# One-hot compares and the coupled sweep's outer-product multiplies, divided along the five tiles of a block

## The chip, the cores and the metric

The kernel runs on one core of a Trainium2 chip. The metric is the device time of one execution in microseconds; lower is better. A program on one core, launched once.

## The reference

Four graph layers follow each other on 12,500 nodes with 32 features (8 scalars and 8 vectors of 3) and 400,000 edges, whose targets `dst` are sorted and whose sources `src` are random. After each layer `x = layernorm(x + layer(x))`.

```python
# layers 0 and 3: weights of each edge from a small network of its own features
w = mlp(edge_features)                       # 4 x 8 x 8 numbers an edge
msg = contract(x[src], edge_harmonics, w)    # 32 numbers an edge
out = segment_sum(msg, dst) + x @ own
...
# layer 1: fixed coupling, harmonics of order 0, 1 and 2 (1 + 3 + 5 = 9 numbers an edge)
msg = sum_paths(W[path], CG[path], sh[path], x[src])
out = segment_sum(msg, dst)
...
# layer 2: two graph convolutions
out = relu(segment_sum(norm * (x @ W)[src], dst) + b)
```

## The kernel before

There are five sweeps over all edges, each followed by a short stage over the nodes: `weighted_edges` (called `weighted0`), `coupled_edges`, `conv_edges` twice, and `weighted_edges` again (called `weighted3`). A program-wide barrier stands between stages. Edges come in blocks of 640, that is 5 tiles (`TILES`) of 128 (`P`), one edge a partition; there are 628 blocks (625 real, padded to 157 turns of `SLOTS` = 4). Since targets are sorted, the targets of one block lie within 64 consecutive nodes (`WINDOW`), so one pass over the blocks is enough for these inputs.

What a block goes through in each sweep:

- SP (`load_blocks`, L301) loads the block's source indices and, where there are any, harmonics and features, into one of four slots. It refills slot s as soon as the messages of that slot's block are made (semaphore `msg_ready`; in the convolutions `spread`).
- POOL (`gather_rows`, L323) issues five indirect DMAs a block, one a tile, that fetch the rows `x[src]` from HBM into `rows[s]`. Each reads a column of indices in SBUF.
- DVE makes a one-hot matrix of each edge's target within the window (`Windows.one_hot`, L359): a compare of `iota` (64 columns) with the local target of the edge, for five tiles in one instruction. It stands at the start of the block's work, ahead of the waits for the gather.
- DVE makes the messages. In `coupled_edges` these are two multiplies: the outer product of the first four harmonics with the 32 features (L701, 5 x 128 columns) and of the other five with the 24 vector features (L705, 5 x 120 columns). In `weighted_edges` there are eleven instructions between the one-hot and `msg_ready` (L576 to L613), of which L594 and L599 read PE's weights in PSUM. In `conv_edges` there are none; PE takes the gathered rows.
- PE multiplies the messages by the one-hot and sums the five tiles in PSUM (L492, L669, L753). In `weighted_edges` PE also makes each edge's weights (L446, L448, L458); there its order is written out by hand: hidden layer of block n + 2, weights of n + 1, then the sum of block n.
- DVE adds the window's sums into the accumulator `acc` in SBUF (`add_window`, L560, L688, L767), at a column that it reads from a register.

All orders are those of the code: each engine's queue runs in program order, and a semaphore count is the only link between engines. DVE's order in a turn of four blocks in `coupled_edges` is: read the bases (L366), then for each slot the one-hot, the wait for gather and loads, the two multiplies, and the add of the block before.

## Time and profile before

| | us |
|---|---|
| time, median of 3 runs | 26496.01 |
| lowest and highest | 26398.16, 26498.13 |
| span of the profiled execution | 21541.2 |
| median less span | 4954.8 |
| busy in the span: PE, DVE, ACT, POOL | 13199.4, 9294.4, 2665.2, 15690.7 |

The span is the time from the first to the last instruction that the profiler recorded in one execution; the profile gives no other time of that execution, so the median stands for it. The times by stage, from the slices of the page: the first weighted sweep takes slices 1 to 8, the coupled sweep 9 to 16, the convolutions 17 to 32, the last weighted sweep 33 to 40. Node stages are short. "Issue" as a releaser means that the engine waited for nothing that the profile shows.

### The profile page before, as it was taken

Reading aid. Unit: us, or ns where it says so; the run is one execution under the profiler, and the core shown is the slowest. Engines: PE = TensorE matmul, PEld = TensorE weight load, DVE = VectorE, ACT = ScalarE, POOL = GpSimd, SP = SyncE. Lnnn points to the kernel's source line nnn. Section 1 sums busy time; section 2 is a strip of 40 time slices with the busy share of each in tenths; the row PEclk is TensorE's granted clock in tenths of the full one; section 3 lists DMA queues with packets and bytes.
Section 4 is the critical chain, followed back from the end, with each engine's and each line's share of the span. In section 5 each row is a group of like instructions: output and inputs, shape, how many; then the busy total and the mean of one; then the engine's idle time right before and its main releaser. Section 6 shows DMA issues by size and latency. Waiting matters only on the chain. (4 is left out here: it accounts for less than half of the span.)

```text
span 21541.2 us, 268058 instructions
## 1 busy us (share of the span) xinstructions
PE 13199.4 (61%) x71680; PEld 9916.4 (46%) x71680; DVE 9294.4 (43%) x22443; ACT 2665.2 (12%) x6512; POOL 15690.7 (73%) x15707
## 2 busy tenths in 40 slices
PE   8999999976666666512222223212221399999999
PEld 5666666666666666511111112111111266666666
DVE  7777777833333333211111111111111388888885
ACT  2333333310000000100000000000000022222222
POOL 6777777747777777677777774777777677777774
PEclk8988988955555555555555555555555599999997
DMA  1111111111111111100000010000000111111111
GB/s 32 26 26 26 26 26 26 27 13 16 16 16 16 16 16 16 15 14 14 14 14 14 14 13 12 14 14 14 14 14 14 15 17 18 18 17 18 17 17 13
DMA packets 1290570, 372.67 MB, mean 17 GB/s; under 512 B 1002127, under 2 KB 1269819, under 8 KB 1290172
## 3 DMA queue, kind: packets, MB, share of 16 engines
q0 software_dynamic: 502400, 258.23, 7.7%
q1 hardware_dynamic: 788150, 114.20, 3.3%
q8 instruction: 8, 0.13, 0.0%
q14 instruction: 12, 0.10, 0.0%
HBM read 363.02 MB, written 8.00 MB: 17 GB/s over the span
## 5 line engine op out<-in xcount | busy, mean ns | idle before, releaser
L323 POOL DMA_INDIRECT conv_rows<-conv_rows,conv_idx x6280 | 5927.4, 944 | 2245.2 <-issue 1912.6
L753 PE MATMUL conv_win<-conv_onehot,conv_rows 128*32 128x64 f32 x12560 | 1572.6, 312 | 6305.3 <-DMA conv_rows<-conv_rows,conv_idx 6254.9
L753 PEld LDWEIGHTS conv_win<-conv_onehot,conv_rows 128*32 128x32 f32 x12560 | 1298.6, 169 | 6579.0 <-issue 4974.1
L323 POOL DMA_INDIRECT coupled_rows<-x_after_weighted,coupled_idx x3140 | 3302.0, 1052 | 1206.1 <-issue 955.0
L323 POOL DMA_INDIRECT weighted_rows<-in_x,weighted_idx x3140 | 3251.5, 1036 | 1105.3 <-issue 937.4
L323 POOL DMA_INDIRECT weighted_rows<-x_after_convolved,weighted_idx x3140 | 3209.0, 1022 | 1064.2 <-issue 953.7
L458 PE MATMUL weighted_weights_ps<-weighted_w_out,weighted_hidden 128*128 128x256 f32 x12580 | 3781.5, 426 | 21.1 <-DVEq L550 21.1
L669 PE MATMUL coupled_win<-coupled_onehot,coupled_prod 128*125 128x64 f32 x12560 | 2762.0, 418 | 1531.0 <-DVE coupled_prod L705 1531.0
L669 PEld LDWEIGHTS coupled_win<-coupled_onehot,coupled_prod 128*125 128x125 f32 x12560 | 2677.4, 330 | 1615.6 <-issue 834.5
L458 PEld LDWEIGHTS weighted_weights_ps<-weighted_w_out,weighted_hidden 128*128 128x128 f32 x12580 | 2256.0, 199 | 1818.0 <-issue 1617.9
L767 DVE TENSOR_TENSOR acc<-acc,conv_win 32x64 f32 x1256 | 262.3, 209 | 6237.3 <-PE conv_win L753 6237.3
L492 PEld LDWEIGHTS weighted_win_ps<-weighted_onehot,weighted_prod 128*128 128x128 f32 (+1 forms) x25120 | 2463.5, 166 | 522.2 <-issue 262.6
L492 PE MATMUL weighted_win_ps<-weighted_onehot,weighted_prod 128*128 128x64 f32 (+1 forms) x25120 | 2542.1, 254 | 242.8 <-DVE weighted_prod L613 241.4
L594 DVE TENSOR_TENSOR weighted_v_v<-weighted_weights_ps,weighted_scaled 128x320 f32<-128x320 f32 x3768 | 1966.0, 577 | 127.0 <-ACT weighted_scaled L520 123.0
L448 PE MATMUL weighted_hid_ps<-weighted_feat,weighted_w_in 32*64 32x320 f32 (+1 forms) x3780 | 1543.6, 489 | 95.9 <-DMA weighted_feat<-in_ef 78.6
L701 DVE TENSOR_TENSOR coupled_prod<-coupled_sh,coupled_rows 128x640 f32<-128x640 f32 x628 | 518.3, 825 | 1726.5 <-DMA coupled_rows<-x_after_weighted,coupled_idx 1726.5
L599 DVE TENSOR_TENSOR weighted_to_s<-weighted_weights_ps,weighted_scaled 128x640 f32<-128x640 f32 x1256 | 1020.6, 813 | 0.0
L446 PE MATMUL weighted_hid_ps<-weighted_first,weighted_w_mid 128*64 128x320 f32 x2520 | 953.3, 460 | 2.8 <-ACT weighted_first L505 2.1
L359 DVE TENSOR_TENSOR conv_onehot<-conv_iota,local 128x320 f32<-128x320 f32 x1256 | 589.8, 490 | 786.0 <-issue 786.0
L508 ACT ACTIVATE weighted_hidden<-weighted_hid_ps,weighted_b_in 64x320 f32<-64x320 f32 x1260 | 657.5, 522 | 1808.6 <-PE weighted_hid_ps L448 1806.4
L520 ACT ACTIVATE weighted_scaled<-weighted_rows,weighted_sh 128x32 f32<-128x32 f32 x3140 | 732.5, 309 | 1133.9 <-DMA weighted_rows<-in_x,weighted_idx 1116.7
L587 DVE TENSOR_TENSOR weighted_s_v<-weighted_weights_ps,weighted_rows 128x320 f32<-128x320 f32 x1256 | 613.6, 489 | 564.2 <-PE weighted_weights_ps L458 554.3
(133 smaller groups left out, 8636.9 us busy)
## 6 DMA issues: line engine op xcount, KB each, us to landing
conv_rows<-conv_rows,conv_idx POOLq DMA_INDIRECT x6280, 2.3
weighted_feat<-in_ef SPq DMA_DIRECT2D x632, 80.0 KB
weighted_rows<-in_x,weighted_idx POOLq DMA_INDIRECT x3140
coupled_rows<-x_after_weighted,coupled_idx POOLq DMA_INDIRECT x3140, 2.3
weighted_rows<-x_after_convolved,weighted_idx POOLq DMA_INDIRECT x3140, 2.3
weighted_idx<-in_src_blocks SPq DMA_DIRECT2D x1264, 2.5 KB
weighted_sh<-in_sh SPq DMA_DIRECT2D x1264, 10.0 KB
conv_idx<-in_src_blocks SPq DMA_DIRECT2D x1264, 2.5 KB, 1.6
```

Of the source, the lines that this page charges most:

```text
L323: pool.indirect_dma_start(rows[s][:, t, :], None, table, bass.IndirectOffsetOnAxis(ap=idx[s][:, t:t + 1].bitcast(U32), axis=0))\
L446: mm = pe.matmul(hid_ps[0:HID, 0:HALF], w_mid[:, u - 1, :], first[:, :], start=True, stop=True)
L448: mm = pe.matmul(hid_ps[0:halves * HID, 0:HALF], w_in[:, :], feat[slot][:, u * HALF:(u + 1) * HALF], start=True, stop=True)
L458: mm = pe.matmul(banks[bank][:, t * WPATHS:(t + 1) * WPATHS], hidden[slot][:, t * P:(t + 1) * P], w_out[:, :], start=True, stop=True)
L492: mm = pe.matmul(win_ps[0:min(P, MSG - c * P), c * WINDOW:(c + 1) * WINDOW], columns, onehot[s][:, t, :], start=(t == 0), stop=(t == TILES ...
L508: step = nc.scalar.activation(hidden[slot][0:HID, half * HALF:(half + 1) * HALF], hid_ps[0:HID, 0:HALF], func, bias=(b_mid if deep else b_ ...
L520: last = nc.scalar.activation(scaled_pair[s % 2][:, t, MUL:], rows[s][:, t, :], ACT.Copy, scale=sh[s][:, t, 0:1])
L587: dve.tensor_tensor(s_v[:, :, :, :], w_sv, x[:, :, None, 0:MUL].broadcast_to([P, TILES, MUL, MUL]), ALU.mult)
L594: last = dve.tensor_tensor(v_v[:, :, m * MUL:(m + 1) * MUL, :], w_vv, v_m[:, :, None, :].broadcast_to([P, TILES, MUL, MUL]), ALU.mult)
L599: dve.tensor_tensor(to_s[:, :, :, :], w_s, scaled[:, :, None, 0:2 * MUL].broadcast_to([P, TILES, MUL, 2 * MUL]), ALU.mult).then_inc(w_used, 1)
L669: mm = pe.matmul(win_ps[s % 2][0:OCH, c * WINDOW:(c + 1) * WINDOW], prod[s][:, t, c * OCH:(c + 1) * OCH], onehot[s][:, t, :], start=(t == ...
L753: mm = pe.matmul(win_ps[s % 2][0:FEAT, 0:WINDOW], rows[s][:, t, :], onehot[s][:, t, :], start=(t == 0), stop=(t == TILES - 1))
```

## The change

`Windows.one_hot`, which all five sweeps call, now issues five `tensor_scalar` compares of 64 columns, one a tile, whose scalar is the column of local targets, in place of one `tensor_tensor` of 5 x 64 columns. In `coupled_edges` each of the two multiplies becomes five, and the two kinds alternate by tile. The values are the same. The semaphore increment moves to the last of the pieces.

```diff
     def one_hot(self, dst, block):
 
-        return self.dve.tensor_tensor(
-            dst[:, :, :], self.iota[:, None, :].broadcast_to([P, TILES, WINDOW]),
-            self.k["local"][:, bass.ds(block, 1), :].rearrange("p b t -> p (b t)")[:, :, None]
-            .broadcast_to([P, TILES, WINDOW]), ALU.is_equal)
+        for t in range(TILES):
+            last = self.dve.tensor_scalar(
+                dst[:, t, :], self.iota[:, :],
+                self.k["local"][:, bass.ds(block, 1), t:t + 1].rearrange("p b t -> p (b t)"), None, ALU.is_equal)
+        return last
...
-                            dve.tensor_tensor(
-                                prod[s][:, :, 0:4 * FEAT].rearrange("p t (c f) -> p t c f", c=4),
-                                h[:, :, 0:4][:, :, :, None].broadcast_to([P, TILES, 4, FEAT]),
-                                x[:, :, None, :].broadcast_to([P, TILES, 4, FEAT]), ALU.mult)
-                            dve.tensor_tensor(
-                                prod[s][:, :, 4 * FEAT:OUTER].rearrange("p t (c f) -> p t c f", c=5),
-                                h[:, :, 4:9][:, :, :, None].broadcast_to([P, TILES, 5, 3 * MUL]),
-                                x[:, :, None, MUL:].broadcast_to([P, TILES, 5, 3 * MUL]), ALU.mult)\
-                                .then_inc(msg_ready, 1)
+                            for t in range(TILES):
+                                dve.tensor_tensor(
+                                    prod[s][:, t, 0:4 * FEAT].rearrange("p (c f) -> p c f", c=4),
+                                    h[:, t, 0:4][:, :, None].broadcast_to([P, 4, FEAT]),
+                                    x[:, t, None, :].broadcast_to([P, 4, FEAT]), ALU.mult)
+                                last = dve.tensor_tensor(
+                                    prod[s][:, t, 4 * FEAT:OUTER].rearrange("p (c f) -> p c f", c=5),
+                                    h[:, t, 4:9][:, :, None].broadcast_to([P, 5, 3 * MUL]),
+                                    x[:, t, None, MUL:].broadcast_to([P, 5, 3 * MUL]), ALU.mult)
+                            last.then_inc(msg_ready, 1)
```

DVE's instructions at the start of a turn of the coupled sweep, the first slot, before. An ISA row is register work of DVE's sequencer, here the address of the block's column of local targets (L359) and the values that the waits compare with (L699, L700).

```order
L359 ISA
L359 TENSOR_TENSOR coupled_onehot<-coupled_iota,local 128x320
L699 ISA
L700 ISA
L701 TENSOR_TENSOR coupled_prod<-coupled_sh,coupled_rows 128x5x128
L705 TENSOR_TENSOR coupled_prod<-coupled_sh,coupled_rows 128x5x120
```

The same place in the changed kernel, from the fourth compare to the second pair of multiplies.

```order
L360 ISA
L360 TENSOR_SCALAR coupled_onehot<-coupled_iota,local 128x64
L360 ISA
L360 TENSOR_SCALAR coupled_onehot<-coupled_iota,local 128x64
L700 ISA
L701 ISA
L703 TENSOR_TENSOR coupled_prod<-coupled_sh,coupled_rows 128x128
L707 TENSOR_TENSOR coupled_prod<-coupled_sh,coupled_rows 128x120
L703 TENSOR_TENSOR coupled_prod<-coupled_sh,coupled_rows 128x128
L707 TENSOR_TENSOR coupled_prod<-coupled_sh,coupled_rows 128x120
```

Three compute instructions of a block have become fifteen. Each of the five compares has register work of its own ahead of it; the ten multiplies have none between them.

DVE in a weighted sweep, from the last multiply of a block to the first of the next, before:

```order
L613 TENSOR_TENSOR weighted_prod<-weighted_sums,weighted_sh 128x5x24
L359 ISA
L359 TENSOR_TENSOR weighted_onehot<-weighted_iota,local 128x320
L576 TENSOR_TENSOR weighted_vsh<-weighted_rows,weighted_sh 128x5x24
```

and in the changed kernel:

```order
L614 TENSOR_TENSOR weighted_prod<-weighted_sums,weighted_sh 128x5x24
L360 ISA
L360 TENSOR_SCALAR weighted_onehot<-weighted_iota,local 128x64
L360 ISA
L360 TENSOR_SCALAR weighted_onehot<-weighted_iota,local 128x64
L360 ISA
L360 TENSOR_SCALAR weighted_onehot<-weighted_iota,local 128x64
L360 ISA
L360 TENSOR_SCALAR weighted_onehot<-weighted_iota,local 128x64
L360 ISA
L360 TENSOR_SCALAR weighted_onehot<-weighted_iota,local 128x64
L577 TENSOR_TENSOR weighted_vsh<-weighted_rows,weighted_sh 128x5x24
```

Here one instruction has become five, each with its register work, between the same neighbours. On PE, ACT, POOL and SP nothing but line numbers differs.

## Rows read from the trace of the kernel before

**Rows 1.** The page: span, busy times, and the granted clock in 40 slices.
```profile
span 21541.2 us, 268058 instructions
...
PE 13199.4 (61%) x71680; PEld 9916.4 (46%) x71680; DVE 9294.4 (43%) x22443; ACT 2665.2 (12%) x6512; POOL 15690.7 (73%) x15707
...
PEclk8988988955555555555555555555555599999997
```

**Rows 2.** Line L323 by tile: ns min/median/max of a gather, first and last start.
```profile
L323 POOL DMA_INDIRECT conv_rows<-conv_rows,conv_idx x6280: 940/944/1164, 8982.9 to 17038.2; - x197
L323 POOL DMA_INDIRECT weighted_rows<-in_x,weighted_idx x3140: 938/945/2619, 58.3 to 4357.5; - x197
L323 POOL DMA_INDIRECT coupled_rows<-x_after_weighted,coupled_idx x3140: 940/944/1597, 4598.5 to 8865.6; - x197
L323 POOL DMA_INDIRECT weighted_rows<-x_after_convolved,weighted_idx x3140: 940/945/2802, 17133.5 to 21311.4; - x197
```

**Rows 3.** Groups by line, whole span: gathers (busy us, mean ns, idle before, releasers).
```profile
L323 POOL DMA_INDIRECT conv_rows<-conv_rows,conv_idx x6280 | 5927.4, 944 | 2245.2 <-issue 1912.6 <-DMA conv_idx<-in_src_blocks 332.6
...
L323 POOL DMA_INDIRECT coupled_rows<-x_after_weighted,coupled_idx x3140 | 3302.0, 1052 | 1206.1 <-issue 955.0 <-DMA coupled_sh<-in_sh 251.2
L323 POOL DMA_INDIRECT weighted_rows<-in_x,weighted_idx x3140 | 3251.5, 1036 | 1105.3 <-issue 937.4 <-DMA weighted_feat<-in_ef 167.9
```

**Rows 4.** Stretches: us; busy (x) of PE, PEld, DVE, ACT, POOL; clock, DMA.
```profile
100.00:2200.00 2100.00, 1988.64 (x10444) 1344.13 (x10443) 1632.11 (x3988) 669.10 (x2150) 1589.24 (x1528) 0.89 0.14 26
...
4630.00:6700.00 2070.00, 1348.65 (x6138) 1307.97 (x6137) 663.01 (x1226) 0.00 (x0) 1603.12 (x1523) 0.50 0.10 16
...
17160.00:19200.00 2040.00, 2038.71 (x11086) 1302.72 (x11085) 1714.98 (x4321) 483.71 (x923) 1562.60 (x1529) 1.00 0.12 17
```

**Rows 5.** Timeline in the coupled sweep (start us, us, what, idle before).
```profile
8009.82 0.49 DVE L359 TENSOR_TENSOR coupled_onehot<-coupled_iota,local 128x320 f32<-128x320 f32 x1 [2.37 <-issue]
8010.23 0.82 DVE L701 TENSOR_TENSOR coupled_prod<-coupled_sh,coupled_rows 128x640 f32<-128x640 f32 x1
8010.36 1.50 POOL L323 DMA_INDIRECT coupled_rows<-x_after_weighted,coupled_idx  x1 [0.30 <-issue]
8010.96 0.78 DVE L705 TENSOR_TENSOR coupled_prod<-coupled_sh,coupled_rows 128x600 f32<-128x600 f32 x1
8011.66 0.49 DVE L359 TENSOR_TENSOR coupled_onehot<-coupled_iota,local 128x320 f32<-128x320 f32 x1
```

**Rows 6.** Timeline, end of a block of the first weighted sweep.
```profile
3009.08 1.71 POOL L323 DMA_INDIRECT weighted_rows<-in_x,weighted_idx  x1 [0.30 <-issue]
3009.14 0.64 DVE L609 TENSOR_TENSOR weighted_prod<-weighted_v_v 128x480 f32<-128x480 f32 x1
3009.71 0.27 DVE L613 TENSOR_TENSOR weighted_prod<-weighted_sums,weighted_sh 128x120 f32<-128x120 f32 x1
```

**Rows 7.** Timeline, last weighted sweep: two short multiplies in a row.
```profile
19005.25 0.28 DVE L576 TENSOR_TENSOR weighted_vsh<-weighted_rows,weighted_sh 128x120 f32<-128x120 f32 x1 [0.55 <-DMA weighted_rows<-x_after_convolved,weighted_idx]
19005.45 0.32 DVE L578 TENSOR_TENSOR weighted_scaled<-weighted_rows,weighted_sh 128x160 f32<-128x160 f32 x1
```

**Rows 8.** Timeline, first convolution sweep: add, then one-hot.
```profile
12013.03 0.21 DVE L767 TENSOR_TENSOR acc<-acc,conv_win 32x64 f32 x1 [2.66 <-PE conv_win L753]
12013.18 0.49 DVE L359 TENSOR_TENSOR conv_onehot<-conv_iota,local 128x320 f32<-128x320 f32 x1
```

**Rows 9.** Timeline, two tensor-scalars in a row, at the end of a sweep.
```profile
4380.21 0.19 DVE L346 TENSOR_SCALAR weighted_iota<-weighted_iota 128x64 f32<-128x64 f32 x1
4380.31 0.47 DVE L347 TENSOR_SCALAR weighted_base_f<-weighted_base_f 1x632 f32<-1x632 f32 x1
```

**Rows 10.** Timeline, a copy beside a gather; and the copies of line L335.
```profile
17155.94 0.94 POOL L323 DMA_INDIRECT weighted_rows<-x_after_convolved,weighted_idx  x1 [0.30 <-issue]
17156.66 0.24 DVE L335 COPY weighted_iota<-iota 128x64 f32<-128x64 f32 x1
...
L335 DVE COPY conv_iota<-iota x2: 118/118/118, 8992.8 to 13128.6; 128x64 f32<-128x64 f32 x2
L335 DVE COPY coupled_iota<-iota x1: 130/130/130, 4621.2 to 4621.2; 128x64 f32<-128x64 f32 x1
```

## The prediction

> **What bounds the kernel now.** I read the page first: POOL has the most busy time, 73% of the span, and PE's clock is at full speed or near it only in the first and last fifth [rows 1]. Shares over five sweeps say little, so the second view was the line of the gathers by tile, whose first and last starts give the length of each sweep [rows 2]. Divided by 628 blocks: first weighted sweep (4357.5 - 58.3)/628 = 6.85 us a block, coupled (8865.6 - 4598.5)/628 = 6.79, last weighted (21311.4 - 17133.5)/628 = 6.65. The convolutions cannot be split from that row, but they have the plain gather, 944 ns, and 1912.6/6280 = 0.305 us of "issue" ahead of each [rows 3], so POOL needs 5 x 1.249 = 6.245 us a block there.
>
> The reader is to see in rows 3 that a gather costs a mean of 944 ns in the convolutions, 1052 in the coupled sweep and 1036 in the first weighted one, while the median is 944 or 945 everywhere and the maximum 1.6 to 2.8 us [rows 2]. A few gathers are long. The timeline shows which [rows 5]: a gather that starts 0.13 us after the multiply L701 takes 1.50 us. It ends at 8011.86, and L701 at 8011.05: 0.81 us later. A normal gather that needed something 0.13 us after its start would have those same 0.81 us left. So the gather wants something of SBUF at about 0.13 us (its indices, I take it), and waits for the end of a DVE multiply that has both its inputs in SBUF. Then it slips in, though L705 follows L701 at once. One such gather a block costs 0.56 us; the group means say (1052 - 944) x 5 = 0.54 us a block, and the sweep says 6.79 - 6.245 = 0.55. **The coupled sweep is POOL's, and 0.55 us of each block (345 us in all) is this wait.** PE has 1399 of 2160 us busy there and DVE 689 [rows 4]; neither bounds it.
>
> The weighted sweeps have the same waits, but other bounds beside them. In the last one PE is busy 2038.71 of 2040 us at the full 2.4 GHz [rows 4]: a faster POOL would only wait for PE. In the first PE is busy 1988.64 of 2100 us at a granted 0.89, so at most 5% is there to win.
>
> **The change, term by term.** The sum is made against the profiled execution, span 21541.2 us; its own time isn't given, and the median of the runs, 26496.01, is 4954.8 us above the span. Nothing in the trace shows what these are. I carry the difference in the span over to the median unchanged.
>
> *Multiplies of the coupled sweep, DVE's time.* Two multiplies of 640 and 600 columns start 0.73 us apart, and the next instruction 0.70 us later [rows 5]: 1.43 us. Two short ones (120 and 160 columns) start 0.20 apart [rows 7]. Ten pieces of 128 or 120 are 10 x 0.20 = 2.0 us: +0.57 us of DVE a block.
>
> *The compare, DVE's time.* One of 320 columns holds DVE 0.41 us (8009.82 to 8010.23, rows 5). For the pieces: two tensor-scalars with no register work between start 0.10 us apart [rows 9]; a 64-column add and the one-hot behind it, with register work for its address between, 0.15 [rows 8]. Each piece has such work, so I take 0.15: 5 x 0.15 = 0.75, +0.34 us a block in all five sweeps (bounds: 5 x 0.10, +0.09; and 5 x 0.20 as in rows 7, +0.59).
>
> *What covers that.* Coupled: DVE is busy 689 of 2160 us, 2.17 us of a 6.79 us block, and +0.91 leaves more than half idle. Convolutions: DVE sat idle for 2.66 us ahead of the add [rows 8], and the compare doesn't wait for the gather; covered. Last weighted sweep: DVE is busy 1714.98 of 2040 us [rows 4], idle 1.06 us a block; +0.34 fits, but at a turn's start, where the bases are read, slack is less. I take 0.03 us a block, +20 us (bounds 0, and all of it, 0.34 x 628 = +214, if DVE's slack were never where it is wanted). If the cover went, PE would wait for L614's messages.
>
> *POOL's wait in the coupled sweep.* With pieces of 0.20 us a gather at its index read (0.13 + 0.13 = 0.26 us after the first multiply) meets the end of the first piece (0.28); over all phases I take 0.10 us. The row of pieces is 0.57 longer, so the next gather, 1.25 us + 0.10 later, reads at 1.61 and meets it too: 0.08. The remainder is 0.18 instead of 0.55: **-0.37 x 628 = -232 us** (bounds: all of it gone, -345; and waits that lengthen, a rival below).
>
> *POOL's wait in the weighted sweeps.* The one-hot is the tail of a row of multiplies, L607 to L359, in which a gather took 1.71 us [rows 6]; five pieces with gaps should let it in sooner. First sweep: -40 us (bounds 0, and the 5% in which PE isn't busy, (2100 - 1988.64)/2100 x 4299 = -228). Last sweep: 0, PE bounds it.
>
> *The compare as a tensor-scalar, POOL's side.* 632 columns in 0.47 us [rows 9] are more than one a cycle of what L701 does (640 in 0.82), so a tensor-scalar in SBUF runs at twice the rate. No gather runs beside those. The nearest rows are copies of the same 128 x 64 shape: beside a gather one took 0.24 us instead of 0.12, and ended as the gather did, while the gather kept its 0.94 [rows 10]. The copy gave way. So I charge POOL little: 0.03 us a block in the three sweeps that POOL bounds alone, 1884 x 0.03 = +57 us (bounds 0, and each of five pieces holding a gather for its 0.10: 942 us).
>
> The Trainium skill ("SBUF — State Buffer", sections "SBUF: two separate sides" and "Who interferes with whom") says that the port pair is an exclusive lock: a two-input VectorE op in SBUF holds off only GpSimd's reads, but a fp32 tensor-scalar in a 2-port mode also holds off the writes of descriptors. By that rule this change swaps a milder lock for a harsher one. Rows 5 agree with its first half; rows 10 show the copy as the loser.
>
> **Sum:** -232 - 40 + 20 + 57 = -195 us, and 26496 - 195 = **26301 us**, 0.7% less. A measurement of this kernel can tell about 0.5%, 132 us, from no change.
>
> **Rivals.** *No change* (23%). The waits shrink less than I think or the compares cost POOL 0.1 us a block (-232 - 40 + 20 + 188 = -64: 26432), or the 4955 us outside the span mean that the timed executions are bound elsewhere, by PE at the 1.2 GHz of the middle stages, for one. For it: that unexplained fifth, and that only one sweep in five has a clean gain. Against it: the three bookkeepings of 0.55 us agree.
>
> *Slower: the gather is refused at every seam* (12%). In rows 6 the gather of 3009.08 ends at 3010.79, 0.81 us after L613's end at 3009.98: it was passed over at the end of L609 (3009.78), where rows 5 let one in. Ten multiplies in a row have nine seams. A gather that is refused at all waits from 0.26 to 2.08 us, 1.82 instead of 0.55: +1.27 x 628 = +798 us, with the other terms 26496 + 798 + 37 = 27331. It decides from a mean wait of 0.55 us on. Against it: L701 and L705 are the very instructions that are divided, and their seam lets gathers in.
>
> *Slower: the compares hold off descriptor writes* (10%). If a gather that meets the row of compares stands still until its end, it loses up to 0.75 us once a block in the POOL-bound sweeps, 1884 x 0.75 = +1413, less 252: 27657. It takes over from 252/1884 = 0.13 us a block. This is what the rule of that page of the Trainium skill would do here. Against it: rows 10, and 0.05 us or more of gap after each compare. A milder form, 0.3 us, gives 26809.
>
> **How the numbers follow.** The forecast has 55%, and its own range is -345 - 228 = -573 to about -130. Low end: most of that, 26020. The two slower cases have 22%; 26900 takes in the milder form and leaves out about 13%. Faster by over 0.5%: 0.55; within: 0.23; slower: 0.22.
>
> **What would show it.** In the changed profile: coupled gathers with a mean near 980 ns instead of 1052 and a sweep of 6.4 us a block; convolution gathers at 944 to 950; compares about 0.19 us each, 0.15 apart; multiplies 0.20 apart; PE of the last weighted sweep still without a gap. The forecast is wrong if convolution gathers are visibly longer than 944, if coupled gathers have a maximum beyond 2 us in numbers, or if the span falls and the time doesn't.

## The result, and the profile after

The changed kernel takes 26700.14 us, median of 4 runs (26653.89 to 26719.16), against 26479.83 us of the kernel before in the same set (26398.16 to 26498.13, 4 runs): ratio 1.0083, interval 1.0062 to 1.0105. It is slower by 0.8%, where I had forecast 0.7% faster. Two more sets gave 1.0076 (1.0057 to 1.0095, e5) and 1.0066 (1.0042 to 1.0090, e17).

The head of the page of the changed kernel:

```profile
span 26717.4 us, 298202 instructions
PE 14457.6 (54%) x71680; PEld 10742.5 (40%) x71680; DVE 11021.9 (41%) x40027; ACT 2634.0 (10%) x6512; POOL 15689.5 (59%) x15707
PE   7888888885555555311111131111112788888888
POOL 4555555537777777566666646666665555555553
PEclk7777777765555555555555555555555888888887
```

The first thing to see is not the change. The span is 26717.4 us, and this execution's time 26719.16. Before, a span of 21541.2 stood beside a median of 26496.01 [rows 1]. POOL's busy time is the same to 2 us (15690.7 there), its share 59% in place of 73%. So the 4955 us that I had "outside the span" lie inside the span of the executions that are timed, as idle time of POOL. My trace of before showed an execution without them. A new trace of the kernel before (e9, 26483.9 us span) is what the change has to be compared with. Its gathers, and those of the changed kernel (columns as in [rows 3]):

```profile
L323 POOL DMA_INDIRECT conv_rows<-conv_rows,conv_idx x6280 | 5961.5, 949 | 3520.1 <-issue 2074.6 <-DMA conv_idx<-in_src_blocks 1445.4
L323 POOL DMA_INDIRECT weighted_rows<-x_after_convolved,weighted_idx x3140 | 3370.5, 1073 | 2344.4 <-DMA weighted_feat<-in_ef 1424.9 <-issue 919.2 <-DMA weighted_sh<-in_sh 0.3
L323 POOL DMA_INDIRECT weighted_rows<-in_x,weighted_idx x3140 | 3213.3, 1023 | 2518.4 <-DMA weighted_feat<-in_ef 1593.5 <-issue 924.6 <-DMA weighted_sh<-in_sh 0.3
L323 POOL DMA_INDIRECT coupled_rows<-x_after_weighted,coupled_idx x3140 | 3123.2, 995 | 2189.9 <-DMA coupled_sh<-in_sh 1254.2 <-issue 934.4 <-DMA coupled_idx<-in_src_blocks 1.3
```

```profile
L323 POOL DMA_INDIRECT conv_rows<-conv_rows,conv_idx x6280 | 5948.6, 947 | 3862.5 <-issue 1972.0 <-DMA conv_idx<-in_src_blocks 1890.5
L323 POOL DMA_INDIRECT coupled_rows<-x_after_weighted,coupled_idx x3140 | 3524.6, 1122 | 1609.4 <-issue 957.0 <-DMA coupled_sh<-in_sh 644.5 <-DMA coupled_idx<-in_src_blocks 7.9
L323 POOL DMA_INDIRECT weighted_rows<-x_after_convolved,weighted_idx x3140 | 3125.1, 995 | 2714.9 <-DMA weighted_feat<-in_ef 1835.6 <-issue 879.3
L323 POOL DMA_INDIRECT weighted_rows<-in_x,weighted_idx x3140 | 3090.3, 984 | 2605.4 <-DMA weighted_feat<-in_ef 1669.2 <-issue 936.2
```

(The first four rows are e9's, the second four those of the changed kernel.) Each row's idle time now has a large part that ends with an SP load: POOL has no block to gather for. In the kernel before that is 1254 us in the coupled sweep; in the changed one it is 645, but each gather there takes 127 ns more: (1122 - 995) x 3140 = 399 us. In the convolutions the wait for loads grows by 445 us, in the last weighted sweep by 411, while its gathers take 78 x 3140 = 245 us less.

Why does POOL run out of blocks? The timeline of e9 in the first convolution (of fourteen gathers in a row four stand here):

```profile
13995.66 0.94 POOL L323 DMA_INDIRECT conv_rows<-conv_rows,conv_idx  x1 [0.30 <-issue]
13995.70 1.25 PE L753 MATMUL conv_win<-conv_onehot,conv_rows 128*32 128x64 f32 x10 [5.03 <-DMA conv_rows<-conv_rows,conv_idx]
13996.91 0.94 POOL L323 DMA_INDIRECT conv_rows<-conv_rows,conv_idx  x1 [0.30 <-issue]
...
14010.65 0.94 POOL L323 DMA_INDIRECT conv_rows<-conv_rows,conv_idx  x1 [0.30 <-issue]
14011.90 0.94 POOL L323 DMA_INDIRECT conv_rows<-conv_rows,conv_idx  x1 [0.30 <-issue]
14015.14 0.33 SPq L301 DMA_DIRECT2D conv_idx<-in_src_blocks  x1
14015.17 0.21 DVE L767 TENSOR_TENSOR acc<-acc,conv_win 32x64 f32 x1 [20.79 <-remote]
14017.50 0.94 POOL L323 DMA_INDIRECT conv_rows<-conv_rows,conv_idx  x1 [4.67 <-DMA conv_idx<-in_src_blocks]
```

The ten matmuls end at 13996.95. Both that wait for their count (`spread`), SP with the refill and DVE with the add, move only at 14015.14: 18.2 us later. POOL has used up its four slots at 14012.84, and the count comes 2.3 us after that. In the trace that I predicted from, the add of [rows 8] starts 0.2 us after the end of its matmuls, and each of the 1256 adds of the convolutions within 0.7 us. I call an add late when it starts over 1 us after the later of the last matmul's end and the end of DVE's instruction before it. Late adds by that count: none of 1884 in the first trace; in e9, 214 of 628 in the coupled sweep (1886 us in sum) and 575 of 1256 in the convolutions (5103 us). In the changed kernel (e5) it is 264 (1483 us) and 792 (6481 us). The profile models the ends of matmuls, so this is lateness against a modelled end: whether the last matmul itself or only its count was held is not told.

The two rows below are waits of the add in the changed kernel (us in sum, times, longest), in the convolutions and in the coupled sweep. "Remote" means that the profile finds no instruction which ended near the count. The row after them is the convolutions' add in a set without late counts (e14), where every wait has PE's matmul as its releaser:

```profile
DVE acc L769 <- remote: 6386.5, 760, 20.8
DVE acc L689 <- remote: 1381.3, 204, 26.2
```

```profile
DVE acc L774 <- PE conv_win L760: 6250.0, 1256, 9.3
```

The weighted sweeps have late counts too. ACT's activation L508 starts over 1 us after the hidden layer's matmul that it needs in 297 of 1254 cases in e9's first weighted sweep (1458 us in sum), in none of 1256 in the first trace. But there they aren't the whole of the difference: between 50 and 5730 us of e9 PE is busy 4610 us at a granted clock of 0.75, between 50 and 4350 us of the first trace 4031 us at 0.90, for the same sweep.

Length of each sweep, from the start of its first gather to the end of its last, in us (the two convolutions added; what is left over is node stages). Sets P measured the kernel before at 26457 to 26517 us, set Q at 27231, set R at 21521; the first trace is like R, its timed runs like P. On record, R is e13 to e16 on chip 0, Q is e1 to e4 on chip 1, and P is e5 to e12 on chip 8 and e17 and e18 on chip 3; for the first trace and the result no chip is given.

| run | set | weighted 0 | coupled | convolutions | weighted 3 | ratio |
|---|---|---|---|---|---|---|
| before, first trace | R-like | 4300 | 4268 | 7841 | 4179 | |
| e9 before | P | 5676 | 5063 | 9149 | 5620 | 0.9994 |
| the change (e5) | P | 5601 | 4890 | 9466 | 5732 | 1.0076 |
| the change (e17) | P | 5678 | 4899 | 9477 | 5740 | 1.0066 |
| e10 outer product only | P | 5662 | 5589 | 9186 | 5679 | 1.0239 |
| e11 compare only | P | 5582 | 5204 | 9452 | 5784 | 1.0187 |
| e1 before | Q | 5729 | 5343 | 9292 | 5900 | 0.9994 |
| e2 outer product only | Q | 5786 | 5822 | 9275 | 5864 | 1.0175 |
| e3 compare only | Q | 5686 | 5259 | 9470 | 5761 | 1.0002 |

Sweeps whose code is the old one show how far two traces differ in sets P: 5605 to 5699 us for the first weighted sweep (seven traces), 5063 to 5084 for the coupled one (three), 9149 to 9186 for the convolutions (three), 5595 to 5679 for the last (seven). In Q it is 57 us for the first weighted sweep (e1, e2). So in sets P the change gains in the coupled sweep and loses in the convolutions and the last weighted sweep, beyond this scatter. In the first weighted sweep it is 5601 to 5678 us over three traces, which shows neither.

Of e16's eight executions one, the profiled one, took 27385 us, the others 21674 to 21773; its trace has no late add in 1884, a coupled sweep of 4321 us, but a first weighted sweep of 8344 us with matmuls of the edge weights at a mean of 816 ns (439 in the first trace), so it is another slowness than that of P and Q.

### The profile page after: what moved, and what is told of

It is laid out like the page before. It is cut to its first block and busy times, and to the rows that moved or that the text cites. A ratio compares the mean times of both kernels' runs of the same rounds, so it can differ in the third digit from the quotient of the medians.

```text
span 26717.4 us, 298202 instructions
## 1 busy us (share of the span) xinstructions
PE 14457.6 (54%) x71680; PEld 10742.5 (40%) x71680; DVE 11021.9 (41%) x40027; ACT 2634.0 (10%) x6512; POOL 15689.5 (59%) x15707
## 5 line engine op out<-in xcount | busy, mean ns | idle before, releaser
L323 POOL DMA_INDIRECT conv_rows<-conv_rows,conv_idx x6280 | 5948.6, 947 | 3862.5 <-issue 1972.0
L323 POOL DMA_INDIRECT weighted_rows<-x_after_convolved,weighted_idx x3140 | 3125.1, 995 | 2714.9 <-DMA weighted_feat<-in_ef 1835.6
L323 POOL DMA_INDIRECT weighted_rows<-in_x,weighted_idx x3140 | 3090.3, 984 | 2605.4 <-DMA weighted_feat<-in_ef 1669.2
L323 POOL DMA_INDIRECT coupled_rows<-x_after_weighted,coupled_idx x3140 | 3524.6, 1122 | 1609.4 <-issue 957.0
L459 PE MATMUL weighted_weights_ps<-weighted_w_out,weighted_hidden 128*128 128x256 f32 x12580 | 4446.9, 486 | 22.5 <-issue 22.5
L459 PEld LDWEIGHTS weighted_weights_ps<-weighted_w_out,weighted_hidden 128*128 128x128 f32 x12580 | 2621.7, 231 | 2243.4 <-issue 1944.4
L493 PEld LDWEIGHTS weighted_win_ps<-weighted_onehot,weighted_prod 128*128 128x128 f32 (+1 forms) x25120 | 2864.7, 187 | 250.1 <-issue 23.8
L493 PE MATMUL weighted_win_ps<-weighted_onehot,weighted_prod 128*128 128x64 f32 (+1 forms) x25120 | 2865.5, 273 | 20.4 <-DVE weighted_prod L614 16.4
L449 PE MATMUL weighted_hid_ps<-weighted_feat,weighted_w_in 32*64 32x320 f32 (+1 forms) x3780 | 1755.8, 550 | 931.0 <-issue 477.7
L447 PE MATMUL weighted_hid_ps<-weighted_first,weighted_w_mid 128*64 128x320 f32 x2520 | 1125.1, 534 | 949.8 <-issue 440.4
L360 DVE TENSOR_SCALAR conv_onehot<-conv_iota,local 128x64 f32<-128x64 f32 x6280 | 1194.6, 277 | 833.7 <-issue 833.3
L360 DVE TENSOR_SCALAR weighted_onehot<-weighted_iota,local 128x64 f32<-128x64 f32 x6280 | 1174.0, 270 | 323.0 <-issue 322.9
L689 DVE TENSOR_TENSOR acc<-acc,coupled_win 125x128 f32 x628 | 180.9, 288 | 2377.1 <-remote 1381.3
```

The source lines that it names most:

```text
L323: pool.indirect_dma_start(rows[s][:, t, :], None, table, bass.IndirectOffsetOnAxis(ap=idx[s][:, t:t + 1].bitcast(U32), axis=0))\
L360: last = self.dve.tensor_scalar(dst[:, t, :], self.iota[:, :], self.k["local"][:, bass.ds(block, 1), t:t + 1].rearrange("p b t -> p (b t)" ...
L447: mm = pe.matmul(hid_ps[0:HID, 0:HALF], w_mid[:, u - 1, :], first[:, :], start=True, stop=True)
L449: mm = pe.matmul(hid_ps[0:halves * HID, 0:HALF], w_in[:, :], feat[slot][:, u * HALF:(u + 1) * HALF], start=True, stop=True)
L459: mm = pe.matmul(banks[bank][:, t * WPATHS:(t + 1) * WPATHS], hidden[slot][:, t * P:(t + 1) * P], w_out[:, :], start=True, stop=True)
L493: mm = pe.matmul(win_ps[0:min(P, MSG - c * P), c * WINDOW:(c + 1) * WINDOW], columns, onehot[s][:, t, :], start=(t == 0), stop=(t == TILES ...
```

## The experiments

**e1, e9: the kernel before.** No edit.

> The kernel before, unchanged, for a second profile and for the size of a null result. Both theories: ratio 1.000 within 0.4%. What it tells: whether its span is 21.5 ms as in the first profile or some 26.5 ms as the timed executions. If the span is 26.5 ms, the first profile showed an execution without stalls that the timed ones have, and the sweeps and the waits have to be read anew from this one.

> The kernel before once more, for a trace on the same chip as the next three. Ratio 1.000 within 0.002. From the runs so far I put its sweeps on a chip of the faster kind (median near 26460) at 5670 (first weighted), 5030 (coupled), 9390 (convolutions), 5660 us (last weighted); on the slower kind (27230) at 5730, 5340, 9510, 5900.

Measured: e1 27228.04 us, span 27248.5; e9 26486.94 us, span 26483.9. The span is the time, and the sweeps are those of the table. Nothing is outside the span.

**e2, e10: the outer product alone.** The second hunk of the change, without the first.

> Only the coupled sweep's multiplies are divided; the compare is the one of before. Theory 1 (the seams between short multiplies let no gather in, so a gather that meets the row waits for its end): all of the loss is here, +150 to +300 us (26630 to 26780), coupled gathers with a mean of about 1120 ns and a maximum near 3 us. Theory 2 (the five compares cost, by DVE time or by their ports): within 60 us of before, coupled gathers at or under 1052 ns.

> Only the outer product divided, again. Theory C (what costs in the whole change is the compare in the convolutions, and the coupled sweep gains a little, as the whole change's sweep of 4890 us against some 5030 suggests): ratio 0.993 to 1.000 on a chip of the faster kind. Theory A' (ten multiplies cost the coupled sweep on any chip): ratio above 1.01 as the first time (1.0175).

Measured: 1.0175 (1.0160 to 1.0189) and 1.0239 (1.0222 to 1.0257). Nearly all of it is in the coupled sweep, +479 and +526 us; the other sweeps, whose code is the old one, differ by up to 59 us. The gathers there have the mean of before (991 ns in e10, 995 in e9), and 9 of 3140 take over 2 us. Theory C, by which the outer product alone would gain, falls. What grew is the wait for loads, from 1254 to 1799 us, behind 305 late adds in place of 214. The row of e10:

```profile
L323 POOL DMA_INDIRECT coupled_rows<-x_after_weighted,coupled_idx x3140 | 3112.4, 991 | 2716.3 <-DMA coupled_sh<-in_sh 1798.7 <-issue 914.1 <-DMA coupled_idx<-in_src_blocks 3.6
```

**e3, e11: the compare alone.** The first hunk without the second.

> Only the compare is divided into five tensor-scalars, in all five sweeps; the multiplies are those of before. Theory 1: within 60 us of before, or up to 100 us faster, since a weighted gather is let in earlier. Theory 2: +150 to +300 us (26630 to 26780), with the convolutions' sweeps longer than in the kernel before.

> Only the compare divided, again. Theory C: the convolutions take 180 to 290 us more, the weighted sweeps together about the same, ratio 1.004 to 1.010. Otherwise 1.0002 as the first time.

Measured: 1.0002 (0.9990 to 1.0015) and 1.0187 (1.0168 to 1.0206). The convolutions are 178 and 303 us longer in the two. In the last weighted sweep the sets differ in sign (-139 and +164), in the coupled one too (-84 and +141); the first weighted sweep is shorter in both (-43, -94), by no more than two traces of one code differ. In sets P each half alone costs about 2%, and both together 0.8%; e11 is outside the 1.004 to 1.010 that I had expected.

The compare does something to the coupled gathers as well. I count the gathers whose read, 0.13 us after the start, falls inside one of the two undivided multiplies. With the old compare ahead of them none passes over the seam between the multiplies (0 of 622 in the first trace, 0 of 374 in e9, 0 of 315 in e1). With the five tensor-scalars ahead 106 of 325 do (e3) and 112 of 409 (e11), and then last up to 2.5 us. A timeline of e11, to be put beside [rows 5], where the gather is let in after the first multiply:

```profile
5920.92 0.90 DVE L360 TENSOR_SCALAR coupled_onehot<-coupled_iota,local 128x64 f32<-128x64 f32 x5
5921.73 0.81 DVE L702 TENSOR_TENSOR coupled_prod<-coupled_sh,coupled_rows 128x640 f32<-128x640 f32 x1
5921.98 2.07 POOL L323 DMA_INDIRECT coupled_rows<-x_after_weighted,coupled_idx  x1 [0.30 <-issue]
5922.47 0.77 DVE L706 TENSOR_TENSOR coupled_prod<-coupled_sh,coupled_rows 128x600 f32<-128x600 f32 x1
```

It ends at 5924.05, 0.81 us after the second multiply.

**e4: the compare in five pieces of the old kind.** Five `tensor_tensor` of 64 columns in place of five `tensor_scalar`.

```diff
-            last = self.dve.tensor_scalar(dst[:, t, :], self.iota[:, :], ..., None, ALU.is_equal)
+            last = self.dve.tensor_tensor(dst[:, t, :], self.iota[:, :], ....broadcast_to([P, WINDOW]), ALU.is_equal)
```

> The compare is divided into five, but each piece is a tensor-tensor of 64 columns, without the double rate; the multiplies are those of before. If a tensor-scalar's ports are what costs, this one is faster than the kernel with the tensor-scalars; if the number of pieces and their DVE time cost, it is as slow or slower (each piece some 0.03 us longer, 0.15 us a block). Theory 1: within 80 us of before, or slower by refused seams, since these pieces also have two inputs in SBUF.

Measured (set Q): 1.0062 (1.0046 to 1.0079). The convolutions take 9491 us, +199 against e1, as with the tensor-scalar (+178); the first weighted sweep is 49 us longer than e1's, within the 57 us of that set. So the cost in the convolutions is the division in five, not the kind of instruction. My third rival, a tensor-scalar that holds off the gathers, has no row for it either: gathers in the convolutions take 947 ns (e3) and 945 (e11), against 953 and 949. In the coupled sweep the kind does count: with the five tensor-tensors ahead 5 of 329 gathers pass over the seam between the multiplies, with the five tensor-scalars 106 of 325 (e3, same set).

**e5, e17: the change again.**

> The changed kernel once more, on the chip and beside the kernel before of this set of runs. If the two halves of the change add up (outer product alone 1.0175, compare alone 1.0002 on a slower chip), the ratio is 1.016 to 1.019. If the compares soften what the multiplies cost (the first measurement of the whole change gave 1.0083), it is about 1.008, and the coupled sweep is shorter than with the outer product alone.

> The changed kernel once more. The last four runs were on a chip where the kernel before takes 21521 us and no count of PE comes late, as in the trace that I predicted from. If this set is on such a chip: first weighted sweep 4223 and coupled 4312 us (as in the last run but two), convolutions within 30 us of 7841, last weighted within 30 of 4179: in sum -60 to +20 us, ratio 0.997 to 1.001, so my -195 us fails there too, on the coupled sweep. If it is on a chip with late counts: 1.007 to 1.010 as twice before.

Measured: both fell in sets P, 1.0076 and 1.0066 (1.0066 lies just under the 1.007 to 1.010 that I had expected). Three of the sweeps are within 12 us of each other, the first weighted one 77 us apart. The effect on the time is stable from set to set within P.

**e6, e12: DVE's time without the division.** In e6 a fill in the coupled sweep, between the waits and the multiplies; in e12 the same with 512 columns ahead of the one-hot in the convolutions.

```diff
                             dve.wait_ge(loaded[s], g * 32 + 32)
+                            dve.memset(scratch[s][:, :], 0.0)      # 600 columns
```

> Before, plus one fill of a scratch tile of 600 columns (about 0.57 us, no input in SBUF) between the waits for the gather and the first multiply of the coupled sweep. It gives DVE the extra time of the ten multiplies and none of their seams. Theory A (in timed executions DVE's time between add and messages is on the path): coupled sweep longer by 300 to 500 us, ratio 1.011 to 1.018, like the outer product alone. Theory B (gathers are refused at seams, the port): ratio within 1.000 to 1.004.

> Before, plus one fill of a scratch tile of 512 columns (about 0.41 us, no input in SBUF) ahead of the one-hot in the convolutions, the same length that five compares add to one. If DVE's time is what the divided compare costs there: convolutions 180 to 290 us longer, ratio 1.007 to 1.011. If it is the number of instructions or their place beside the gathers: convolutions within 80 us, ratio 0.997 to 1.003.

Measured: e6 0.9960 (0.9948 to 0.9972), with the coupled sweep 4940 us, 123 less than e9, though its gathers take 1063 ns in place of 995; late adds 209 (1667 us). e12 1.0014 (1.0002 to 1.0026), convolutions 9174, +25. As much DVE time as the ten multiplies add makes the sweep shorter, and as much as the compares add costs next to nothing, though the convolutions' gathers take 985 ns beside the fill in place of 949. Theory A, that DVE's time is on the path, falls; e6 lies outside Theory B's 1.000 to 1.004 too.

**e7, e8: adds three blocks behind.** In the coupled sweep and the convolutions the add of block n - 3 follows the messages of block n, with four PSUM banks; e8 has the divided outer product too.

```diff
-                            if s > 0:
-                                add_window(n - 1, s - 1, bases[s - 1])
-                        add_window(g * SLOTS + (SLOTS - 1), SLOTS - 1, bases[SLOTS - 1])
+                        if not first:
+                            add_window(n - LAG, (s - LAG) % SLOTS, bases[s])
```

> Before, with the window's add three blocks behind the one-hot and the messages in the coupled sweep and the convolutions (it was one block behind, and none at a turn's end), and four PSUM banks in place of two. Theory A (PE's late counts hold DVE, and through it PE and POOL): the coupled sweep and the convolutions lose most of their stalls; coupled about 4400 us in place of 5300, convolutions about 8300 to 8900 in place of 9500, ratio 0.93 to 0.97. Theory B (the stalls come from gathers or loads themselves): ratio 0.99 to 1.01.

> The kernel with the adds three blocks behind, plus the divided outer product (no divided compare). Theory A: with the slack the extra 0.57 us of DVE is covered, so against the one without it the coupled sweep is within 100 us, and my first sum's gain of up to 232 us can show. Theory B: the divided outer product costs its 450 to 480 us here too.

Measured: 0.9984 (0.9970 to 0.9997) and 1.0056 (1.0036 to 1.0075). For e7 Theory A had 0.93 to 0.97. The slack that should have swallowed the late counts brought 70 us in the coupled sweep (4993) and lost 37 in the convolutions (9186). POOL still runs dry, since in the convolutions SP's refill waits for the same count, and in the coupled sweep PE itself goes slowly at times. Among the twenty matmul records of a block of the coupled sweep, starts over 0.6 us apart are found nowhere in the first trace, 158 times in e9 (228 us in sum) and 1641 times in e7 (2556 us). What the slack took from DVE's waits came back as slow starts on PE. In the rows below, of e8, its instructions start 1.4 to 2.8 us apart, while the normal distance is 0.21. The divided outer product costs 152 us in that sweep here (5145), not 526.

```profile
7018.89 0.94 POOL L324 DMA_INDIRECT coupled_rows<-x_after_weighted,coupled_idx  x1 [0.30 <-issue]
7018.95 0.26 PE L667 MATMUL coupled_win<-coupled_onehot,coupled_prod 128*125 128x64 f32 x1 [2.53 <-issue]
7021.76 0.27 PE L667 MATMUL coupled_win<-coupled_onehot,coupled_prod 128*125 128x64 f32 x1 [2.54 <-issue]
...
7023.89 0.94 POOL L324 DMA_INDIRECT coupled_rows<-x_after_weighted,coupled_idx  x1 [0.30 <-issue]
...
7029.45 10.77 PE L667 MATMUL coupled_win<-coupled_onehot,coupled_prod 128*125 128x64 f32 x51 [0.44 <-issue]
```

POOL's last gather ends at 7024.83. From 7029.45 on PE makes 51 matmuls in 10.77 us.

**e13: the divided outer product and a fill.** 512 columns ahead of the one-hot, in the coupled sweep.

> The outer product divided (alone: ratio 1.0239, coupled sweep 5589 us against 5063), plus a fill of 512 columns (about 0.41 us) ahead of the one-hot in the coupled sweep, where the divided compare would add the same time. Theory D (what a piece costs hangs on where in a gather PE's matmuls end, so its time only shifts that moment): the added work makes it faster, coupled sweep 4850 to 5200 us, ratio 0.993 to 1.008. If DVE's time is the cost: slower still, above 1.024. If the tensor-scalar compares did it and not their time: as the outer product alone, 1.022 to 1.026.

Measured: 0.9986 (0.9967 to 1.0005), but in set R, where before takes 21520.76 us and no add is late. Coupled sweep 4260 us against 4268. The question, whether added time undoes the cost of the outer product where counts are late, stays open. What it says of R: there the ten multiplies with that fill cost nothing, and none of the 3140 gathers takes over 1.72 us.

**e14: the change kept where it had gained.**

```diff
-                            win.one_hot(onehot[s], i * SLOTS + s).then_inc(vec, 1)
+                            win.one_hot(onehot[s], i * SLOTS + s, name == "weighted0").then_inc(vec, 1)
```

`one_hot` has the five compares if its last argument is true, as it is in the coupled sweep too, and the one compare otherwise.

> The change kept in the coupled sweep (compare and outer product) and its compare in the first weighted sweep; the old compare in the convolutions and the last weighted sweep. If each sweep's time depends on its own code alone: first weighted 5600, coupled 4895, convolutions 9150, last weighted 5640 us, in sum 240 to 260 us less than before, ratio 0.990 to 0.992, better than both kernels.

Measured, set R: 0.9983 (0.9963 to 1.0003), where I had 0.990 to 0.992 from the sweeps of P. By the sweeps of sets P it should be the fastest there; that was not measured. Its trace is of the longest of its executions (21664.53 us; median 21492.19), in which the last weighted sweep, whose code is the old one, took 4321 us. The first weighted sweep took 4223 us, 77 less than in the first trace, the coupled one 4312, 44 more.

**e15: half the fill.** As e6, with 300 columns.

> Before, with a fill of 300 columns (about 0.27 us) in place of the one of 600 ahead of the first multiply of the coupled sweep (600 gave 4940 us for the sweep against 5063). If more slack of time were simply good or bad, it lies between, 4970 to 5040. Theory D: the times don't follow the size in order; anything from 4850 to 5500 us, outside that band more likely than in it.

Measured, set R: 1.0065 (1.0044 to 1.0086); coupled sweep 4406 us, 138 more than the first trace, with gathers of a mean of 1095 ns. 514 of the 3140 gathers take over 1.6 us, none in the first trace (maximum 1597, [rows 2]). A fill of a quarter of a microsecond, on an engine that is idle for more than half the time, costs 0.65% of the kernel. In 473 of the 514 the fill is running at the gather's read, and the gather ends 0.81 us after the end of the multiply behind the fill.

**e16, e18: POOL waits for the count.** In the convolutions, ahead of a block's fourth gather, for the add of the block before.

```diff
             for t in range(TILES):
+                if summed is not None and t == 3:
+                    hold(pool, summed, g * SLOTS + s + 1, started)
                 pool.indirect_dma_start(...)
```

> Before, with POOL waiting ahead of the fourth gather of each convolution block until the window of the block before is added, which is just when PE has finished it. Theory D (a count of PE that meets a running gather is held up, and comes soon after POOL stops): adds later than 6 us after the last matmul nearly vanish (575 of 1256 adds are over 1 us late in the kernel before, a tenth over 13.5 us), and POOL loses 2 to 5 us at each late one; convolutions 8900 to 10500 us. If the lateness has nothing to do with POOL, waits of 13 us and more stay as they are and the convolutions take over 11000 us.

> The kernel in which POOL waits ahead of the fourth gather of each convolution block for the add of the block before. On a chip with late counts: if a count that meets a running gather is held up until POOL stops, adds later than 6 us nearly vanish and the convolutions take 8900 to 10500 us against 9150; if POOL has nothing to do with it, waits of 13 us and more stay. On a chip without: convolutions 8035 us against 7841, ratio 1.008 as before, and nothing new.

Measured: e16 in set R 1.0077 (1.0049 to 1.0104), nothing to learn on late counts; its convolutions take 8035 us, 194 more than the first trace, which is what the added wait costs where no count is late. e18 in a set P: 0.9997 (0.9982 to 1.0011), convolutions 9188 us. Of 1256 adds **none is later than 6 us** (313 in e9), the latest is 4.2 us late (20.6 in e9), the sum 1236 us (5103). The coupled sweep, which isn't changed, is as it was: 5067 us, 214 late adds. In the timeline of e18:

```profile
14004.33 1.24 PE L755 MATMUL conv_win<-conv_onehot,conv_rows 128*32 128x64 f32 x10 [4.98 <-DMA conv_rows<-conv_rows,conv_idx]
14004.33 0.94 POOL L325 DMA_INDIRECT conv_rows<-conv_rows,conv_idx  x1 [0.30 <-issue]
14005.58 0.94 POOL L325 DMA_INDIRECT conv_rows<-conv_rows,conv_idx  x1 [0.30 <-issue]
14009.12 0.21 DVE L769 TENSOR_TENSOR acc<-acc,conv_win 32x64 f32 x1 [9.36 <-remote]
14010.14 0.94 POOL L325 DMA_INDIRECT conv_rows<-conv_rows,conv_idx  x1 [3.61 <-DVE acc L769]
```

The matmuls end at 14005.57, POOL stops at 14006.52, and the add comes at 14009.12, 2.6 us after POOL stopped. Where POOL has to stop for the count, the long lateness is gone. Two limits of this: stopping POOL also stops the transfers of its gathers, whose last packet ends 1.1 us after the gather, so the run doesn't tell the two apart; and a count doesn't need POOL to stop. In e9's convolutions 338 of the 575 late adds start while POOL is still issuing gathers at its normal pace, 102 of the 313 later than 6 us among them, and in the coupled sweep of the change (e5) only 24 of 264 start after POOL has been idle for over 1 us.

There is no gain in it: POOL idles 1043 us for the add instead of 1110 us for loads (1445 less 335, the rows of e9 and e18). The sum of lateness fell by 3867 us and the time stayed, with 194 us that the added wait costs anyway: that sum isn't time lost.

```profile
L325 POOL DMA_INDIRECT conv_rows<-conv_rows,conv_idx x6280 | 5925.6, 944 | 3597.0 <-issue 2200.3 <-DVE acc L769 1043.4 <-DMA conv_idx<-in_src_blocks 335.0
```

## Why the prediction was wrong

**The step that failed first** is the sentence "I carry the difference in the span over to the median unchanged". A fifth of the time was missing from my trace. It was no overhead beside the kernel but a bound of its own, which the trace didn't have: PE's completion counts come up to 20 us late in the executions that are timed. There POOL isn't busy 73% of the time but 59%, and a sweep's length isn't that of its gathers alone. In the kernels of sets P that have the add where it was, the coupled sweep's length goes with the sum of late adds:

| | late adds, sum us | coupled sweep, us |
|---|---|---|
| the change, e5 | 1483 | 4890 |
| e6 fill | 1667 | 4940 |
| e9 before | 1886 | 5063 |
| e11 compare only | 2060 | 5204 |
| e10 outer product only | 2625 | 5589 |

(e12 and e18, whose coupled sweep is the old one, have 1906 and 5084, 1861 and 5067.) This is a correlation between traces of one kind of set: e7 has more lateness, 2528 us, with 4993 us. I had this under "no change", as a sentence on executions that "are bound elsewhere, by PE at the 1.2 GHz of the middle stages": the place was wrong as well. The granted clock of the coupled sweep is 0.50 in the first trace [rows 4] and 0.50 in e10 too, 1.2 GHz in both.

**The multiplies, DVE's time**: right. They start 0.20 us apart; the row of ten lasts 2.06 us. **The compare**: five last 0.40 us longer than one (0.81 us from the first to the multiply, 0.41 before); I took 0.34.

**"Covered"**: right as DVE's time (e6, e12, e13), and no help. An engine with cover can still move the moment at which others meet. The 1399 and 689 us of 2160 that the prediction gives to [rows 4] are of the sweep's other half, 6700 to 8860 us; the row shown has 1349 and 663 of 2070, the same shares.

**POOL's wait in the coupled sweep**, -232 us: wrong by itself, in set R too, where my trace holds. e14 has both parts there and took 44 us more, gathers at a mean of 1065 ns, where I had forecast about 980. The failing point is "a gather at its index read meets the end of the first piece": many do, but not all. The timeline of the changed kernel, first and last pieces of a row of ten:

```profile
7007.47 0.28 DVE L703 TENSOR_TENSOR coupled_prod<-coupled_sh,coupled_rows 128x128 f32<-128x128 f32 x1
7007.68 0.28 DVE L707 TENSOR_TENSOR coupled_prod<-coupled_sh,coupled_rows 128x120 f32<-128x120 f32 x1
7007.71 2.64 POOL L323 DMA_INDIRECT coupled_rows<-x_after_weighted,coupled_idx  x1 [0.30 <-issue]
...
7009.06 0.28 DVE L703 TENSOR_TENSOR coupled_prod<-coupled_sh,coupled_rows 128x128 f32<-128x128 f32 x1
7009.26 0.28 DVE L707 TENSOR_TENSOR coupled_prod<-coupled_sh,coupled_rows 128x120 f32<-128x120 f32 x1
```

This gather ends at 7010.35, 0.81 us after the last piece's end at 7009.54, the same 0.81 as in [rows 5]. It was passed over at every seam that was left. Gathers over 2 us in the coupled sweep: none of 3140 in the first trace and in e9, 120 in e14, 283 in e17, which is my rival "refused at every seam" for part of the gathers. In e14 those 120 cost 173 us over a plain gather, and all others 208 us where the first trace has 338: a gain of 130 us, not 232, and a loss above it. The short multiplies alone don't explain the refusals: with the old compare ahead of them 9 gathers of 3140 are over 2 us in e10, 1 in e2 and none in e13, so the five tensor-scalars ahead have a part in them, as they have with the undivided multiplies of e3 and e11. They aren't the only way to it: e8, with the old compare and the adds moved, has 132. My argument against that rival, that the seam of L701 and L705 lets gathers in, holds only behind the old compare, and with the adds moved not quite there (27 of 437 pass over the seam in e7).

Where counts are late the long gathers cost 399 us, outweighed there by 610 us less waiting for loads. That the coupled sweep of the change is 173 us shorter than before in e5 and e9, near the forecast 232, is luck: it comes from the waits for loads, which the sum doesn't have.

**The weighted sweeps**: -40 in the first. The mechanism held for the gathers: a mean of 985 ns (e5) against 1023 (e9). In R the sweep took 4223 us (e14) against 4300 in the first trace and 4271 and 4273 in e13 and e15, 48 to 77 less; in P the change's three traces (5601 to 5678) aren't told apart from those of the old code (5605 to 5699). The last one I put at +20 as PE's own; in P it is +112 (e5), though its gathers are 78 ns shorter. POOL waits for loads 411 us more. No run in R has the divided compare there.

**The compares beside the gathers**, +57: wrong mechanism. Gathers of the convolutions stay at 944 to 947 ns. Yet the convolutions carry most of the loss, +317 us in e5, where POOL's wait for loads grows and late adds go from 575 to 792. This is the term that makes the sign wrong where the kernel is timed: I had called the compare's DVE time covered and priced only POOL's gathers. Why a compare in five pieces makes more counts late is not shown; e4 and e12 show that it's the division, not the kind of instruction and not the time. The Trainium skill ("SBUF — State Buffer", "Who interferes with whom") has the fp32 tensor-scalar, in a 2-port mode, holding off descriptor writes; no gather of the convolutions shows it, and e4's tensor-tensors cost the convolutions as much.

**Rows of my watch-list**: compare spacing 0.16 us, multiplies 0.20, convolution gathers 947, as written. Coupled gathers 1122 and a maximum of 2980 were the named signs of error, and so was a span that doesn't tell the time.

## What stays open

Shown: PE's counts are late in sets P and Q, they are so while POOL issues gathers, and where POOL is made to stop for them none is over 4.2 us late (e18). In e9's convolutions 567 of 1132 last matmuls that ended while POOL was issuing had a late add, and 8 of 124 that ended with POOL idle. The moment within a gather has no fixed meaning. In e9's coupled sweep, of 173 last matmuls that ended 0.38 to 0.75 us into a gather 72% had a late add, of 324 within its first 0.25 us 13%; in its convolutions it is the other way about, 30% of 211 and 66% of 230. That fills, seams and divisions act by moving such moments fits these counts, but is not shown, and it doesn't yield the sign for a given edit.

Late counts and slow starts may be one thing, since the slack of e7 turned waits for the one into the other; no run tests it. Not settled: what holds the counts, whether POOL's instructions or their transfers matter, why R has none of it (it is the one set on chip 0, but a set on that chip in the other condition is missing), why five tensor-scalars change which seam a gather takes, and why the two halves of the change cancel in the coupled sweep.

## What to carry to other kernels

When the median and the span of the profile differ by more than a per cent, the trace shows another execution than the one that is timed; find what the difference is before any sum is made, or forecast "unknown". Where two engines work on the same block through semaphores, an edit that is covered still shifts who meets whom: test it against a filler of the same length at the same place. Dividing an instruction to open seams for another engine gains only if the seams are taken, and here 120 to 285 of 3140 gathers waited over a microsecond at such a row where none had before. What stands ahead of the row can decide it, as the kind of compare did here.

## What the hardware showed that I hadn't expected

- The same kernel before took 21521 us in one set, 26457 to 26517 in four, 27231 in one, each within 0.9% inside a set. POOL's busy time is 15690.7 us in the first trace and 15669.3 in e9, so the whole difference is idle time of POOL; late counts stand behind it, and in the weighted sweeps a PE that is busy for longer at a lower granted clock as well.
- A count of PE reached DVE and SP together up to 20 us after the last matmul's end, while POOL issued up to 13 gathers of 0.94 us at their normal pace; the count came 2.3 to 2.6 us after POOL stopped in the two rows shown, and often while POOL was still issuing (338 of 575 late adds of e9's convolutions).
- In the same sets PE at times started one instruction each 0.7 to 2.8 us (e8), at the same granted clock of 0.50 as when it ran normally.
- A gather beside short two-input multiplies 0.20 us apart waited for the rest of the row of ten (2.64 us in place of 0.94).
- Five tensor-scalars of 64 columns ahead of two long multiplies let 106 of 325 and 112 of 409 waiting gathers pass over the seam between them; with one tensor-tensor ahead it was 0 of 622 and 0 of 374, with five 5 of 329.
